# A mixture-of-experts kernel on one core: sixteen slots for expert tiles in place of eight

## The reference, cut to what matters

```python
x = x + gnn(layernorm(x), adj, ...)        # x: 4096 x 128, adj: 4096 x 4096, float32
xf = layernorm(x)
logits = xf @ Wr + br                      # 64 experts
top, idx = top_k(logits, 2)
gates = softmax(top)
for e in range(64):                        # W1: 128 x 256, W2: 256 x 128 for each expert
    y = relu(xf @ W1[e] + b1[e]) @ W2[e] + b2[e]
    out = out + combine[:, e:e+1] * y      # combine: the two gates of each token, else 0
x = x + out
```

## Time and profile before

| | |
|---|---|
| median of 3 runs (lowest, highest) | 396.17 us (394.76, 397.02) |
| profiled execution | 396.82 us |
| its span, first to last instruction | 395.0 us |
| busy: PE, DVE, ACT, POOL | 86%, 76%, 42%, 56% of the span |
| DMA, mean | 302 GB/s |
| mean granted TensorE clock | 0.954 of full speed |

### The profile page before, as it was taken

How to read it: one execution, slowest core, us unless ns; L and a number is a source line. 1 busy time by engine, 2 the same in 40 slices (tenths; PEclk the granted TensorE clock), 3 DMA queues, 4 the chain that set the end, 5 groups by cost and what they waited for, 6 DMA issues and landing times.

```text
span 395.0 us, 8459 instructions
## 1 busy us (share of the span) xinstructions
PE 341.3 (86%) x2076; PEld 282.6 (72%) x2076; DVE 301.6 (76%) x923; ACT 166.0 (42%) x267; POOL 220.9 (56%) x221
## 2 busy tenths in 40 slices
PE   4999898998999999999998976997999999999100
PEld 1446685885886868868787965886999999999100
DVE  3879779879799899898994746975777777767067
ACT  2575565646764865648622212111222122212063
POOL 4360002048887848668574754566677777777500
PEclk9899999999999999999999996999999999999655
DMA  8999999998996979969965182787999999995097
GB/s 307 361 425 386 347 425 381 375 428 321 424 383 247 420 283 362 401 247 416 386 267 216 44 259 80 217 243 231 308 289 306 298 312 280 298 280 165 25 371 267
DMA packets 45625, 119.28 MB, mean 302 GB/s; under 512 B 7705, under 2 KB 19630, under 8 KB 37410
## 3 DMA queue, kind: packets, MB, share of 16 engines
q1 hardware_dynamic: 29090, 97.21, 66.2%
q10 hardware_dynamic: 11520, 13.26, 11.2%
q0 software_dynamic: 4992, 8.54, 5.9%
HBM read 104.02 MB, written 16.78 MB: 306 GB/s over the span
## 4 chain that ended last, share of the span: by engine, by line
PE 44%; DVE 29%; DMA 14%; ACT 8%; issue 3%; SPq 1%; POOLq 0%; DVEq 0%; POOL 0%; ACTq 0%
DVE adj_low L769 14%; PE bank L1064 10%; PE bank L1186 10%; DMA adj_ring<-adj_t 8%; PE bank_pair L1200 5%; PE bank L1200 5%; ACT adj_high L640 4%; ACT payload L655 3%; PE bank L1180 3%; PE bank_pair L1197 3%; PE bank L1197 2%; PE bank L1082 2%; DVE x_sb L1002 2%; DMA expert_answers<-adj_ring,ans 2%; DMA x_sb<-x 2%
## 5 line engine op out<-in xcount | busy, mean ns | idle before, releaser
L769 DVE TENSOR_TENSOR adj_low<-adj_ring,adj_high 128x2048 fp32r<-128x2048 f32 x47 | 106.9, 2286 | 15.7 <-ACT adj_high L640 15.2
L580 POOL DMA_INDIRECT dispatched_rows<-payload,slot x64 | 91.5, 1430 | 48.0 <-DMA dispatched_rows<-pad_rows 17.9
L640 ACT CAST adj_high<-adj_ring 128x2048 fp32r<-128x2048 f32 x47 | 89.5, 1906 | 53.8 <-DMA adj_ring<-adj_t 32.7
L588 POOL DMA_INDIRECT expert_answers<-adj_ring,ans x92 | 90.4, 983 | 37.8 <-ACT adj_ring L698 19.7
L1078 PE MATMUL bank<-adj_high,z_hi 128*128 128x512 f32 (+1 forms) x200 | 79.5, 401 | 0.7 <-ACT adj_high L640 0.7
L1079 PE MATMUL bank<-adj_high,z_lo 128*128 128x512 f32 (+1 forms) x200 | 74.7, 378 | 0.0
L1064 PE MATMUL bank<-adj_ring,z_sb 128*128 128x128 f32 (+2 forms) x240 | 64.7, 421 | 4.3 <-DVE z_sb L755 4.3
L966 DVE TENSOR_SCALAR adj_ring<-bank,adj_ring 128x128 f32<-128x128 f32 x184 | 56.0, 345 | 12.8 <-PE bank L1186 10.5
L1186 PE MATMUL bank<-xt_sb,adj_ring 128*128 128x128 f32 x368 | 57.2, 279 | 0.2 <-DVE xt_sb L956 0.2
L1064 PEld LDWEIGHTS bank<-adj_ring,z_sb 128*128 128x128 f32 x240 | 36.5, 194 | 25.4 <-issue 23.5
L1082 PE MATMUL bank<-adj_low,z_hi 128*128 128x512 f32 (+1 forms) x200 | 50.7, 378 | 0.2 <-DVE adj_low L769 0.2
(11 more groups left out here) (154 smaller groups left out, 419.9 us busy)
## 6 DMA issues: line engine op xcount, KB each, us to landing
adj_ring<-adj_t SPq DMA_DIRECT2D x64, 1024.0 KB, 9.0
adj_ring<-w_pack SPq DMA_DIRECT2D x52, 257.5 KB
adj_ring<-w_pack ACTq DMA_DIRECT2D x40, 257.5 KB
dispatched_rows<-pad_rows SPq DMA_DIRECT2D x8, 528.0 KB, 11.4
adj_ring<-expert_answers SPq DMA_DIRECT2D x8, 512.0 KB, 6.9
adj_ring<-dispatched_rows SPq DMA_DIRECT2D x52, 66.0 KB
adj_ring<-dispatched_rows ACTq DMA_DIRECT2D x40, 66.0 KB
out<-x_sb SPq DMA_DIRECT2D x8, 256.0 KB, 4.4
```

The lines of the kernel that those rows point to most:

```text
L580: pool.indirect_dma_start(rows, bass.IndirectOffsetOnAxis(ap=slot[:, b, t, k:k + 1], axis=0), payload[:, b, t, k, :], None).then_inc(scatt ...
L588: pool.indirect_dma_start(y_tok, bass.IndirectOffsetOnAxis(ap=ans[:, s:s + 1], axis=0), y_sb[:, s, :], None, bounds_check=N * K - 1, oob_i ...
L640: nc.scalar.copy(high[:, m % PARTS], adj_sb[:, slot_of(g, k)]).then_inc(hi_ready, 1)
L769: v.tensor_tensor(low[:, m % PARTS], adj_sb[:, slot_of(g, k)], high[:, m % PARTS].bitcast(F32), ALU.subtract).then_inc(lo_ready, 1)
```

## The change

The number of slots goes from 8 to 16, so that the 16 early tiles fill one turn. The slots' rows and 15 of the weights lie in the chunk ring, the 16th slot's weights, the hidden values and the answers in `z_sb`, which is free after the first stage. SyncE loads all 16 early tiles, weights and rows together, after one wait for the scatter of the full groups, each with a wait for the last chunk that used its part of the ring. After that SyncE loads slots 0 to 7 of each turn and ScalarE slots 8 to 15; loads wait for `down` of the tile 16 earlier. The first turn of 16 tiles is written out on each engine, and the loops turn over 16 slots with a test for each of four quads. `relu` waits for the scatter of the tile 16 earlier. The diff, cut to its core:

```diff
-SLOTS = 8
-SP_SLOTS = 4
+SLOTS = 16
+QUADS = SLOTS // QUAD
+SP_QUADS = QUADS // 2
-EARLY = 2 * SLOTS
+EARLY = SLOTS
-OCTETS = (EARLY + REST_CAP) // SLOTS
+TURNS = (EARLY + REST_CAP) // SLOTS
...
-        w_sb = in_ring(SLOTS * WCOLS, "p (s c) -> p s c", s=SLOTS)
         xin = in_ring(SLOTS * ROW, "p (s c) -> p s c", s=SLOTS)
+        in_z = z_sb[:].rearrange("p t f -> p (t f)")
+        w_sb, w_end = [], []
+        for _ in range(SLOTS - 1):
+            w_sb.append(in_ring(WCOLS, "p c -> p c"))
+            w_end.append(taken)
...
+        w_sb.append(in_z[:, 0:WCOLS])
+        w_end.append(RING * CJ * GN)
-        h_sb = in_ring(DEEP * HC * P, "p (b c t) -> p b c t", b=DEEP, c=HC)
-        y_sb = in_ring(SLOTS * D, "p (s f) -> p s f", s=SLOTS)
+        h_sb = in_z[:, WCOLS:z_h].rearrange("p (b c t) -> p b c t", b=DEEP, c=HC)
+        y_sb = in_z[:, z_h:z_y].rearrange("p (s f) -> p s f", s=SLOTS)
...
             sp.wait_ge(early_table_ready, 1)
-            starts = load_starts(SP, early_table, 0, SLOTS)
-            sp.wait_ge(chunk_used, chunk_no(GROUPS - 1, 0))
-            for s in range(SLOTS):
-                load_weights(sp, starts[s], s)
             wait_full_scattered(sp)
-            for s in range(SLOTS):
-                load_rows(sp, starts[s], s)
-            starts = load_starts(SP, early_table, SLOTS, SP_SLOTS)
-            for s in range(SP_SLOTS):
-                next_tile(starts[s], 0, s)
+            for half in range(QUADS):
+                starts = load_starts(SP, early_table, half * QUAD, QUAD)
+                for n in range(QUAD):
+                    last_chunk = CHUNKS * CHUNKS - RING + (w_end[half * QUAD + n] - 1) // (CJ * GN)
+                    sp.wait_ge(chunk_used, max(last_chunk + 1, chunk_no(GROUPS - 1, 0)))
+                    load_tile(sp, starts[n], half * QUAD + n)
             sp.wait_ge(table_ready, 1)
             quads = quads_in_use(sp)
             wait_all_scattered(sp)
-            with sp.Fori(1, OCTETS - 1) as turn:
...
+            with sp.Fori(0, TURNS - 1) as turn:
+                for half in range(SP_QUADS):
+                    with sp.If(turn * QUADS + (half + QUADS) < quads):
+                        starts = load_starts(SP, table, turn * SLOTS + half * QUAD, QUAD)
+                        for n in range(QUAD):
+                            next_tile(starts[n], turn, half * QUAD + n)
...
-            act.wait_ge(early_table_ready, 1)
...
-            starts = load_starts(ACTIVATION, early_table, SLOTS + SP_SLOTS, SLOTS - SP_SLOTS)
-            for s in range(SLOTS):
+            for s in range(SP_QUADS * QUAD):
                 copy_y(0, s)
-                if s >= SP_SLOTS:
-                    load_tile(act, starts[s - SP_SLOTS], s)
             act.wait_ge(table_ready, 1)
             quads = quads_in_use(act)
             wait_all_scattered(act)
...
+            def copy_quad_and_load(turn, half):
+                starts = load_starts(ACTIVATION, table, turn * SLOTS + half * QUAD, QUAD)
+                for n in range(QUAD):
+                    copy_y(turn, half * QUAD + n)
+                    load_tile(act, starts[n], half * QUAD + n)
+
+            for half in range(SP_QUADS, QUADS):
+                copy_quad_and_load(0, half)
+            with act.Fori(1, TURNS) as turn:
+                for half in range(QUADS):
+                    if half < SP_QUADS:
+                        with act.If(turn * QUADS + half < quads):
+                            copy_quad(turn, half)
+                    else:
+                        with act.If(turn * QUADS + (half + QUADS) < quads):
+                            copy_quad_and_load(turn, half)
+                        with act.If(turn * QUADS + (half + QUADS) >= quads):
+                            with act.If(turn * QUADS + half < quads):
+                                copy_quad(turn, half)
...
-            with pool.Fori(1, OCTETS) as turn:
-                for half in range(2):
-                    with pool.If(turn * 2 + half < quads):
+            with pool.Fori(1, TURNS) as turn:
+                for half in range(QUADS):
+                    with pool.If(turn * QUADS + half < quads):
```

More of the change, by code:

```diff
@@ L275, in program @@
         skip_tab = sb("skip_tab", [P, EARLY + P + 1])
-        table = sb("table", [2, P], I32)
+        table = sb("table", [2, P + SLOTS], I32)
         early_table = sb("early_table", [1, EARLY], I32)
@@ L368, in quads_in_use @@
         def quads_in_use(eng):
[L369 removed]
+            return eng.value_load(table[1:2, 0:1], min_val=2 * QUADS, max_val=(EARLY + REST_CAP) // QUAD)
         def load_starts(engine, starts, first, tiles):
@@ L408, in ahead @@
             run(range(start, alike), False)
-            with eng.If(turn * 2 + (half + 1) < quads):
+            with eng.If(turn * QUADS + (half + 1) < quads):
                 run(range(alike, end), True)
-            with eng.If(turn * 2 + (half + 1) >= quads):
+            with eng.If(turn * QUADS + (half + 1) >= quads):
                 run(range(alike, end), False)
@@ L496, in _ @@
             wait_all_scattered(sp)
-            with sp.Fori(1, OCTETS - 1) as turn:
[L498 to L502, removed]
-                        for s in range(QUAD, SP_SLOTS):
-                            next_tile(starts[s], turn, s)
+            with sp.Fori(0, TURNS - 1) as turn:
[4 more added lines that the diff above has]
+                            next_tile(starts[n], turn, half * QUAD + n)
             for s in range(SLOTS):
-                sp.wait_ge(y_out[s], ((quads + (1 if s < QUAD else 0)) // 2) * 16)
+                sp.wait_ge(y_out[s], ((quads + (QUADS - 1 - s // QUAD)) // QUADS) * 16)
             answers = y_tok.rearrange("(p t k) f -> p t k f", p=P, k=K)
@@ L707, in _, with copy_quad @@
             wait_all_scattered(act)
-            def copy_octet(turn):
-                for half in range(2):
-                    with act.If(turn * 2 + half < quads):
-                        for s in range(half * QUAD, half * QUAD + QUAD):
-                            copy_y(turn, s)
-            with act.Fori(1, OCTETS - 1) as turn:
-                with act.If(turn * 2 + 3 < quads):
-                    starts = load_starts(ACTIVATION, table, turn * SLOTS + (SLOTS + SP_SLOTS - EARLY), SLOTS - SP_SLOTS)
-                    for s in range(SLOTS):
-                        copy_y(turn, s)
-                        if s >= SP_SLOTS:
-                            load_tile(act, starts[s - SP_SLOTS], s)
-                with act.If(turn * 2 + 3 >= quads):
-                    copy_octet(turn)
-            copy_octet(OCTETS - 1)
+            def copy_quad(turn, half):
+                for s in range(half * QUAD, half * QUAD + QUAD):
+                    copy_y(turn, s)
+            def copy_quad_and_load(turn, half):
[16 more added lines that the diff above has]
+                                copy_quad(turn, half)
             act.wait_ge(gates_done, 1)
@@ L992, in _ @@
             quads = quads_in_use(dve)
-            with dve.Fori(1, OCTETS) as turn:
-                for half in range(2):
-                    with dve.If(turn * 2 + half < quads):
+            with dve.Fori(1, TURNS) as turn:
+                for half in range(QUADS):
+                    with dve.If(turn * QUADS + half < quads):
                         ahead(dve, turn, half, quads, steps)
@@ L1221, in _ @@
             quads = quads_in_use(pe)
-            with pe.Fori(1, OCTETS) as turn:
-                for half in range(2):
-                    with pe.If(turn * 2 + half < quads):
+            with pe.Fori(1, TURNS) as turn:
+                for half in range(QUADS):
+                    with pe.If(turn * QUADS + half < quads):
                         ahead(pe, turn, half, quads, steps)
```

16 lines of the change are left out of this document (9 added, 7 removed).

## The result

The kernel after takes 399.68 us (median of 4 runs, 399.06 to 400.31), the kernel before 395.93 beside it (4 runs, 394.76 to 397.02): ratio 1.0089, 95% interval 1.0062 to 1.0117. The forecast was 395.4 with a range of 392 to 398, so it was wrong, in sign and in range. The profiled execution of after took 399.06, span 397.2.

The account below looks back on a forecast made before the run. GpSimd's scatters, one per 1.288 us, were taken to bound the kernel. New holes of 4.4 for 5.2 gain 0.8: 396.0 on the profile's base, 395.4 on the median's, range 392.0 to 398.0.

Parts of the forecast that it names:

- sum of new holes: GpSimd's scatters after the change: new holes of 1.3 + 2.1 + 1.0 = 4.4 us replace 5.2, gain 0.8.
- The stall: TensorE waits about 3.5 us for rows of tiles 20 to 23, bounds 0 and 5.5; 2.1 reach GpSimd.
- up to tile 12: GpSimd's holes from ScalarE's late copies: 0.8 at tile 8 and 0.5 at tile 12, 1.3 us.
- Together 5.2: GpSimd's holes before the change at tiles 8, 16 and 24 (1.93, 1.83, 1.48), 5.2 us to win.
- GpSimd's loop entry is hidden as before, under a running scatter.: GpSimd entering its loop after the written-out first turn was to cost nothing.
- 0.3 and 0.7: Holes in us at tiles 24 and 28 from ScalarE reading starts, 1.3 to 1.5 each.
- the lag: GpSimd due later than its copies allow: swallows 1.4 us of the wait for rows, then is gone.
- Early loads, VectorE, the last stage: Sixteen early tiles arrive with five us slack; VectorE no longer waits for scatters; final stage unchanged: no cost or gain.
- No crowd: Faster rival: transfers of the first table tiles keep up with need, 3.9 us won, 392.3; chance 0.34.
- crowd: SyncE's tiles 16 to 23 and ScalarE's 24 to 31 share transfers: 16 tile loads asked for in 11 us.
- Code fetched anew in each turn: Slower rival: doubled loop bodies make VectorE or TensorE fetch code in each of five turns, 398.4; chance 0.08.
- The slower side: All outcomes slower than no change that shows, up to 399 us; chance 0.13.

Follow-up runs that it names:

- before_again: The kernel before, unchanged, run and profiled a second time: 396.10 us (1 run).
- after_again: The kernel after, unchanged, timed and profiled a second time: 400.66 us (median of 6 runs), ratio 1.0124 to the kernel before.
- known_starts: Kernel after, with the start addresses of tiles 24 to 31 in ScalarE's registers before copy 0 and the length read after copy 15: 401.58 us, ratio 1.0128.
- code_shift: Kernel after, with 40 waits on a full semaphore added on ScalarE before copy 0 to push its later code further: 399.51 us (1 run).
- order_of_need: Kernel after, with each turn's loads dealt alternately by quads, SyncE slots 0-3 and 8-11, ScalarE the others: 397.22 us, ratio 1.0046 to before.

## Why the prediction was wrong

On the profile's own base the forecast was 396.0, and the profiled execution of after took 399.06, 3.1 more. Of these, 2.7 are the sum of new holes, 7.1 for 4.4, and 0.3 is the later scatter 5. The stall is not what was too small in that sum (1.84 for 2.1 on GpSimd); the delays of ScalarE and GpSimd themselves were: 0.6 more up to tile 12, 0.9 at 15 and 16 and 1.0 at 31 and 32 that had no term, 0.45 more at 24 and 28.

- **"Sum of new holes 4.4."** This step failed first: measured 7.1 and 6.1. Up to tile 12: 1.9 for 1.3, ScalarE's second reading and tile 9. The stall itself was right in place and near in size: 3.0 and 3.7 us of waits for 3.5, at tiles 19 to 21 for 20 to 23, with GpSimd's hole there 1.84 for 2.1. It was right for partly wrong reasons: the transfers ran at 383 GB/s, not 322, but SyncE asked for the rows of tile 23 at 268.81 where I had it done by 267.
- **"Together 5.2", what the change can win.** This step failed too. The 5.2 were those of one execution, in which TensorE had waited 2.9 us for rows and one start on SyncE took 2.08. In before_again the waits are 0.5 and 2.35 is left, nearly all of it ScalarE's loop entry at 8. That hole gives GpSimd a lag of 2, under which the late copy 24 costs nothing; in the first execution, behind a stall of TensorE, it cost 1.48. From the second execution (396.10) the forecast's own new holes give an estimate of 396.10 - 2.35 + 4.4 = 398.2, slower.
- **"GpSimd's loop entry is hidden as before, under a running scatter."** Wrong in the first execution: 0.60 at tile 16, idle by "issue", and 0.27 at 15, still ahead of the loop; in after_again, behind a hole of 0.56 at 13, only 0.14 at 16. Before, it lay inside the hole at 8.
- **"0.3 and 0.7" at 24 and 28.** Measured 0.39 and 1.06, and 1.03 more at 31 and 32 behind the start of 1.34. As the prediction said, the lag is gone behind the stall; what it lacked is that all of ScalarE's later delays then show.
- **The clock** was in no term. In the first profile the stall was followed by a granted clock of 0.71 and 0.86, 4 x 0.29 + 4 x 0.14 = 1.7 us of full speed at most; in known_starts by 0.64, in code_shift by 0.60; in after_again it was not. So it comes on top in some executions. The record lists the mean granted clock of every timed run: in after_again 0.947 to 0.957 in the three faster ones and 0.939 to 0.940 in the three slower (401.28 to 403.96), in order_of_need 0.953 in the fastest and 0.937 in the slowest. In these two series the slower runs have less clock; whether it made them slow, and in which stretch they lost it, no trace shows.
- **Early loads, VectorE, the last stage:** as said. First weights at 231.49, no wait on tiles 0 to 15, no wait of VectorE for scatters, last stage 23.1 in both.
- **The rivals.** No crowd falls; but with the crowd mostly taken out, order_of_need took 395.2 in the profiled execution, not 392.3: its holes are 2.9 and not 1.3, and its scatter 5 came 0.6 later. Code fetched anew in each turn falls too: in 300 to 372 no instruction queue moved a packet. The rule of the Trainium skill ("Runtime: NRT & Kernel Launch", Instruction fetch mechanics) thus has no case in the later turns here. The slower side came by a crowd that was no worse than forecast, with more of ScalarE's and GpSimd's own delays around it, against a kernel before that had less to win.

Between the medians stand 3.75 and 5.06 us; between the sums of holes, two executions of each, 6.6 - 3.8 = 2.8. The rest is not resolved by four profiles: those of after are the fastest of their series, and between the profiled times themselves (399.06 and 398.36 against 396.82 and 396.10) stand 2.25.

## What to carry to other kernels

When two queues are filled at the same time, deal the loads out by order of need: the same loads, dealt to the two engines in turn, took out 2.5 of the 3.75 us between the medians, half of the loss by the ratios. Before a hole is priced as a gain, look at a second execution: a stall by chance and the holes it uncovers can make up half of it. And holes on an engine that is only 5% slower than its feeder don't add: each makes a lag that hides the next, until a stall takes it.

## What the hardware showed that I had not expected

With both load queues full the transfers moved 383 GB/s (268 to 276), above the 322 of the early loads. Starts of loads that take 0.7 to 2.1 us in place of 0.33 came at times in pairs, on both queues within 0.4 us of each other (268.45 and 268.81 in after; 270.61 and 270.49 in code_shift), and every start of 1.0 us or more, 29 in 14 executions, lies within 0.5 us of the beginning of a packet on an instruction queue. A stall with TensorE busy for 1.57 of 4 us was followed by the lower clock, and one with 2.05 (code_shift), but one with 2.01 (after_again) was not.
